# Attention: issue orders of TensorE, ScalarE and VectorE written over two pairs of units, and 1920 columns masked by GpSimd in place of 1792

## The reference, cut to what matters

```python
scores = jnp.einsum('bhqd,bhkd->bhqk', q / math.sqrt(HEAD_DIM), k)
scores = scores + attention_bias
scores = jnp.where(src_mask, -jnp.inf, scores.astype(jnp.float32))
probs = jax.nn.softmax(scores, axis=-1).astype(v.dtype)
ctx = jnp.einsum('bhqk,bhkd->bhqd', probs, v)
```

## Time and profile before

| | us |
|---|---|
| median of 3 runs | 3619.0 |
| the profiled execution | 3623.18 |
| its span, first to last instruction | 3621.4 |
| PE busy (share of the span) | 3559.3 (98%) |
| VectorE busy | 2256.5 (62%) |
| ScalarE busy | 2184.5 (60%) |
| GpSimd busy | 2062.6 (57%) |
| mean granted TensorE clock | 0.993 of full speed |

### The profile page before, as it was taken

The page is one execution under the profiler, slowest core; times in us unless marked ns, Lnnn a source line. Parts: engine busy times, 40 slices in busy tenths (PEclk is TensorE's granted clock), DMA queues, the critical chain, the costliest instruction groups (busy, mean ns, idle before and its releaser), DMA issues. The chain is left out here.

```text
span 3621.4 us, 79854 instructions
## 1 busy us (share of the span) xinstructions
PE 3559.3 (98%) x32051; PEld 2451.5 (68%) x32051; DVE 2256.5 (62%) x4503; ACT 2184.5 (60%) x3047; POOL 2062.6 (57%) x782
## 2 busy tenths in 40 slices
PE   7999999999999999999999999999999999999998
PEld 3444468888888888888888888887544444444444
DVE  7676668888888888888888888887211111111102
ACT  2343369999999999999999999998210210110110
POOL 1111169898899989899998899996310110120100
PEclk8999999999999999999999999999999999999999
DMA  5555598888998888988888988887300110111002
GB/s 190 202 186 185 189 394 326 320 332 322 349 371 322 322 321 331 379 339 325 321 321 335 387 330 321 322 320 262 139 24 11 35 35 11 40 55 39 20 24 93
DMA packets 210118, 828.62 MB, mean 229 GB/s; under 512 B 25044, under 2 KB 58964, under 8 KB 134488
## 3 DMA queue, kind: packets, MB, share of 16 engines
q1 hardware_dynamic: 204532, 815.09, 59.7%
q10 hardware_dynamic: 5220, 8.42, 0.6%
HBM read 732.19 MB, written 91.23 MB: 227 GB/s over the span
## 5 line engine op out<-in xcount | busy, mean ns | idle before, releaser
L1196 POOL TENSOR_TENSOR at_tiles<-at_tiles,at_negmask 128x1792 f32<-128x1792 f32 x509 | 1827.8, 3634 | 191.9 <-DMA at_tiles<-in_bias 178.8
L1286 ACT ACTIVATE at_tiles<-at_tiles,at_rmin 128x2048 f32<-128x2048 f32 x512 | 1025.3, 2002 | 58.2 <-DVE at_rmin L1333 57.6
L1232 PE MATMUL at_ps_p<-consts,at_tiles 128*128 128x128 f32 x8192 | 1024.9, 272 | 0.1
L1232 PEld LDWEIGHTS at_ps_p<-consts,at_tiles 128*128 128x128 f32 x8192 | 929.8, 141 | 37.8 <-ACT at_prob_t L1294 0.6
L1294 ACT ACTIVATE at_prob_t<-at_ps_p 128x512 f32<-128x512 f32 x1536 | 831.5, 596 | 128.7 <-PE at_ps_p L1232 127.1
L1333 DVE CUSTOM_DVE_ANT_0 at_tiles<-at_ps_s,at_tiles 128x1024 f32<-128x1024 f32 x512 | 624.7, 1220 | 119.2 <-PE at_ps_s L1213 112.4
L1213 PE MATMUL at_ps_s<-at_k_stack,at_q_stack 128*128 128x512 f32 x2048 | 677.4, 432 | 6.0 <-DVE at_rmin L1333 4.1
L1333 DVE CUSTOM_DVE_ANT_0 at_tiles<-at_ps_s,at_tiles,at_rmin 128x1024 f32<-128x1024 f32 x512 | 657.8, 1285 | 18.8 <-PE at_ps_s L1219 0.5
L1249 PE MATMUL at_ps_c<-at_prob_t,at_v 128*32 128x128 f32 x16384 | 500.3, 274 | 0.6 <-DVE at_ctx_rows L1351 0.6
L1249 PEld LDWEIGHTS at_ps_c<-at_prob_t,at_v 128*32 128x32 f32 x16384 | 431.6, 110 | 43.7 <-issue 43.0
L1710 PE MATMUL ff_ps_m<-ff_w,ff_hid 128*128 128x512 f32 x1024 | 441.8, 593 | 0.0
(11 more groups left out here) (193 smaller groups left out, 2635.3 us busy)
## 6 DMA issues: line engine op xcount, KB each, us to landing
at_tiles<-in_bias SPq DMA_DIRECT2D x512, 1024.0 KB, 7.0
at_k_stack<-k_hi SPq DMA_DIRECT2D x128, 256.0 KB, 5.1
at_k_stack<-k_lo SPq DMA_DIRECT2D x128, 256.0 KB, 5.3
negm<-em_mask_out SPq DMA_DIRECT2D x32, 512.0 KB, 6.6
at_q_stack<-q_hi SPq DMA_DIRECT2D x128, 128.0 KB, 5.1
at_q_stack<-q_lo SPq DMA_DIRECT2D x128, 128.0 KB, 5.2
at_v<-v SPq DMA_DIRECT2D x64, 256.0 KB, 7.8
at_negmask<-negm SPq DMA_DIRECT2D x32, 512.0 KB, 9.7
```

What stands on the lines that cost most here:

```text
L1196: pool.tensor_tensor(tiles[s][:, 0:PCOLS], tiles[s][:, 0:PCOLS], negm[s][:, 0:PCOLS], ALU.add).then_inc(s_pool, 1)
L1232: last = pe.transpose(ps_p[k][:, y * P:(y + 1) * P], tiles[s][:, t * P:(t + 1) * P], ident)
L1286: act.activation(tiles[s][:, :], tiles[s][:, :], ACT.Exp, bias=rmin[:, s, 1:2], scale=-1.0, accum_out=rsum[:, s:s + 1]).then_inc(s_exp, 1)
```

## The change

The width of GpSimd's masking grows from 1792 to 1920 columns, in the embedding stage too, and TensorE's mask matmul shrinks from 256 to 128 columns. The loop bodies of the three engines now cover two pairs, four units (g counts them, u = 4g, pr = 2g), from g = -1; what falls outside the range of units is skipped by a test at the head of each helper. TensorE runs a unit's scores four units ahead of its transposes. V (`pv`) stands before the last chunk of a unit's transposes, with the second half of one unit's scores and the first half of the next behind it. ScalarE takes 13 of 16 chunks, VectorE 3. The tests (`if not 0 <= u < NU: return`, and the same with pr and NP), one in each of the eleven helpers, are left out of the diff here except for the first.

```diff
--- before.py
+++ after.py
...
 
     at = Parts()
     at.early = 3
-    at.pool_columns = S - 256
+    at.pool_columns = S - 128
     at.k_st, at.q_st, at.v_sb, at.tiles, at.negm = [None] * 2, [None] * 2, [None] * 2, [None] * RING, [None] * RING
 
     def kqv(i):
...
     B, S = net.B, net.S
     QB = S // P
     RING = 8
-    PCOLS = S - 256
+    PCOLS = net.at.pool_columns
     HALF = S // 2
     SPAN = RING * P
     QH = S // SPAN
...
             stack = net.consts[:, C_STACK:C_STACK + 2 * HD]
 
             def qk(u, a):
+                if not 0 <= u < NU:
+                    return
                 n, s, b, qh, h = place(u)
                 if s == 0 and a == 0:
                     pe.wait_ge(s_kin[n % 2], 64 * (n // 2 + 1))
...
                 last.then_inc(s_pv, 1)
 
             def parts_sum(pr):
                 pe.wait_ge(s_cxs, pr + 1)
                 pe.matmul(ps_c[:, P:P + 2 * HD], cx_sb[:], stack, start=True, stop=True).then_inc(s_cxm, 1)
 
-            for u in range(2):
-                qk(u, 0)
-                qk(u, 1)
-            for p in range(NP + 2):
-                u = 2 * p
-                if u + 2 < NU:
-                    qk(u + 2, 0)
-                    qk(u + 2, 1)
-                if p >= 2:
-                    parts_sum(p - 2)
-                if p < NP:
-                    transposes(u, (0, 1))
-                    if u + 3 < NU:
-                        qk(u + 3, 0)
-                    transposes(u, (2, 3))
-                    transposes(u + 1, (0,))
-                    if u + 3 < NU:
-                        qk(u + 3, 1)
-                    transposes(u + 1, (1, 2, 3))
-                if 1 <= p <= NP:
-                    pv(p - 1)
+            for g in range(-1, NU // 4 + 1):
+                u, pr = 4 * g, 2 * g
+                transposes(u, (0, 1))
+                qk(u + 3, 1)
+                parts_sum(pr - 2)
+                transposes(u, (2, 3))
+                qk(u + 4, 0)
+                transposes(u + 1, (0, 1, 2))
+                pv(pr - 1)
+                qk(u + 4, 1)
+                qk(u + 5, 0)
+                transposes(u + 1, (3,))
+                transposes(u + 2, (0, 1))
+                qk(u + 5, 1)
+                parts_sum(pr - 1)
+                transposes(u + 2, (2, 3))
+                qk(u + 6, 0)
+                transposes(u + 3, (0, 1, 2))
+                pv(pr)
+                qk(u + 6, 1)
+                qk(u + 7, 0)
+                transposes(u + 3, (3,))
 
         @block.scalar
         def _(act):
             cxv = net.ctx.rearrange("(b q t p) c -> (b q) p t c", p=P, t=RING, q=QH)
 
             def exp(u):
                 s = u % RING
                 act.wait_ge(s_sc, 2 * u + 2)
                 act.activation(tiles[s][:, :], tiles[s][:, :], ACT.Exp, bias=rmin[:, s, 1:2], scale=-1.0,
                                accum_out=rsum[:, s:s + 1]).then_inc(s_exp, 1)
 
             def take(u, c):
                 k, i = bank(u, c)
                 pr, j = divmod(u, 2)
                 after(act, s_pv, pr - 1)
...
                                ACT.Copy).then_inc(s_pe[k], 1)
 
             def store(pr):
                 if (pr // 4) % HEADS == HEADS - 1:
                     act.wait_ge(s_cxo, pr + 1)
                     of = slice(2 * (pr % 4), 2 * (pr % 4) + 2)
                     act.dma_start(cxv[pr // (4 * HEADS)][:, of, :], cx_all[:, of, :]).then_inc(s_st[pr % 4], 16)
 
-            exp(0)
-            for p in range(NP + 3):
-                u = 2 * p
-                if 1 <= p <= NP:
-                    take(u - 1, 1)
-                if p < NP:
-                    exp(u + 1)
-                    for c in range(3):
-                        take(u, c)
-                    if u + 2 < NU:
-                        exp(u + 2)
-                    take(u + 1, 2)
-                    take(u + 1, 3)
-                if p >= 3:
-                    store(p - 3)
+            for g in range(0, NU // 4 + 1):
+                u, pr = 4 * g, 2 * g
+                take(u - 2, 2)
+                take(u - 2, 3)
+                exp(u)
+                take(u - 1, 1)
+                exp(u + 1)
+                take(u - 1, 3)
+                take(u, 0)
+                take(u, 1)
+                take(u, 2)
+                take(u, 3)
+                exp(u + 2)
+                take(u + 1, 1)
+                take(u + 1, 2)
+                exp(u + 3)
+                take(u + 1, 3)
+                take(u + 2, 0)
+                take(u + 2, 1)
+                store(pr - 3)
+                store(pr - 2)
+            store(NP - 1)
             for i in range(RING // 2):
                 act.wait_ge(s_st[i], 16 * B * QH)
 
...
                                 rinv[:].unsqueeze(2).broadcast_to([P, 2, HD]), ALU.mult).then_inc(s_cxo, 1)
 
             def parts(pr):
                 dve.wait_ge(s_pv, pr + 1)
                 v.tensor_copy(cx_sb[:], ps_c[:, 0:P]).then_inc(s_cxs, 1)
 
-            for u in range(2):
-                scores(u, 0)
-                scores(u, 1)
-            scores(2, 0)
-            for p in range(NP + 2):
-                u = 2 * p
-                if u + 2 < NU:
-                    scores(u + 2, 1)
-                if p >= 2:
-                    context(p - 2)
-                if p < NP:
-                    take(u, 3)
-                    take(u + 1, 0)
-                if u + 3 < NU:
-                    scores(u + 3, 0)
-                    scores(u + 3, 1)
-                if 1 <= p <= NP:
-                    parts(p - 1)
-                if u + 4 < NU:
-                    scores(u + 4, 0)
+            for g in range(-1, NU // 4 + 1):
+                u, pr = 4 * g, 2 * g
+                context(pr - 2)
+                scores(u + 3, 1)
+                scores(u + 4, 0)
+                take(u + 1, 0)
+                parts(pr - 1)
+                scores(u + 4, 1)
+                scores(u + 5, 0)
+                context(pr - 1)
+                scores(u + 5, 1)
+                scores(u + 6, 0)
+                take(u + 3, 2)
+                take(u + 3, 0)
+                scores(u + 6, 1)
+                parts(pr)
+                scores(u + 7, 0)
 
 
 def ffn_stage(nc, net):
```

More of the change, by code:

```diff
@@ L1235, in pv @@
             def pv(pr):
+                if not 0 <= pr < NP:
+                    return
                 n = pr * 2 // RING
```

## The result

The changed kernel takes 3608.8 us, the median of 6 runs, against 3619.65 for the kernel before on the same chip: a ratio of 0.9969, 95% interval 0.9959 to 0.9978, which is 8 to 15 us saved. The forecast was 3611, 8 us less than before; measured are 11 us less.

A forecast was written before the change was run, and what follows sets the result against it. PE was taken to bound attention, with two resources close behind. Terms -19 + 0 + 4 + 7 = -8 took the profiled 3623.2 to 3615, on the median 3611 us; own range 3602 to 3618, whole range 3584 to 3632.

The forecast's parts named there:

- The loop PE, DVE, PE: Attention, each pair: PE's score weight load waits for DVE's minimum; new order removes about 0.075 us a pair, -19 us.
- the tightest place: New attention order: scores(u+7,0) on DVE, parts queued ahead, finish 0.15 us before PE wants them for qk(u+8,0).
- The narrower mask at 0: PE's mask matmul in attention: 128 fewer columns save 0 us; other end 0.053 per mask, -27 us.
- GpSimd: Masking in attention: 1920 columns take 3.90 us, 3.86 a unit back to back, under PE's 3.93; steady-state cost 0.
- The start, +4: Start of attention: looking four units ahead costs 4 us, bounds 0 and 7.
- the two reasons given: Start of attention: POOL no longer catches up; transposes end 14.4 us after their scores begin instead of 10.8.
- The mask reloads, +7: After each of three mask reloads in attention, tiles land late for the scores: 7 us, bounds 3 and 15.
- of which DVE's idle time takes 0.4: After mask reloads: DVE's idle time absorbs only 0.4 us of the 1.8 and 3.9 us shortfalls.
- the 3.9 us by which tiles were to be late: After the third mask reload: masked tiles 3.9 us short of their scores, from 3.2 us of room before.
- the 6.6 and 0.5 taken off: Room between masking and scores after reloads: 6.6 us less from looking further ahead, 0.5 for two longer maskings.
- The starving ring: Rival, chance 0.17: a head's second bias tile comes late, DVE's scores wait in each head; +24 us, 3635.
- The chance of 0.21 for slower: Whole kernel: chance of a measurably slower result, from ring starvation and a quarter of the case where the wait moves.

## Why the prediction was right, and where its terms were off

**The loop PE, DVE, PE** (the step -19). Right: the pair went from 7.93 to 7.86, the wait is what the orders removed, and moving one line removes it too (3606.75). It was a little too large: 0.065 us a pair on the average, 17 us. The term had a bound of 0 because I gave the tightest place 0.15 us. The trace has 0.43 there, and the run with the longer parts bears it out. The error is in VectorE's durations, each a little long: 0.10 in the second half of scores ahead of parts (1.20 for 1.30), 0.09 in parts (0.21 for 0.30), 0.05 in the first half up to its minimum (1.22 for 1.27); the rest is in the layout. The 1.27 of the earlier trace rows is the distance to the unit's own second half, which by the program waits for the first half's minimum. In the new order other work stands between the two, and behind a first half it starts after 1.15.

**The narrower mask at 0.** Right: the run with the old width has the same time, and where a transpose follows a mask the same change saves 0.05 each (3606.1 in the old order, 3582.0 with both masks). So what decides is what follows the mask. That it is the length of the next weight load fits the load records, which were the right row to go by since the distance of 0.12 could not tell; no run varied the load alone. Of the two statements of the Trainium skill ("TensorE: Matmul & The Clock Gate") that I set beside it, the 107 ns for any 128 columns of weights (section LDWEIGHTS) would have made 0 of both masks in every order. A transpose right behind a mask at 0.07 speaks against it for these transposes' weights; that mask and sum take 0.29 at either width agrees with it for the others.

**GpSimd.** 3.87 us measured for 3.90, waiting 14.7 us of 600, no bound. Right.

**The start, +4.** The size was near, and of the two reasons given one was right. Counting transposes in the trace, unit 4's first starts 24.0 us after the first score matmul before, 27.2 after, and 26.9 in the new orders with the old width. So of the 3.2 us GpSimd's catching up has 0.3 at most. The rest came with the orders and is near the other reason, transposes that end 14.4 us behind the start of their scores in place of 10.8, 3.6 us later. The waits of 488 to 560 us show VectorE waiting for GpSimd 13.1 us in the changed kernel:

```profile
DVE at_tiles L1357 <- POOL at_tiles L1196: 13.1, 11, 3.7
```

**The mask reloads, +7.** Much too dear; this is the term that failed. The ring did lose room (the late reads show how little is left), and after the first reload VectorE does wait for GpSimd, 7.5 us in 982 to 1045. But TensorE hardly lost anything:

```profile
DVE at_tiles L1357 <- POOL at_tiles L1196: 7.5, 8, 1.4
```

```profile
1000.22 1.48 PE L1236 MATMUL at_ps_p<-consts,at_tiles 128*128 128x128 f32 x12
...
1063.62 1.47 PE L1236 MATMUL at_ps_p<-consts,at_tiles 128*128 128x128 f32 x12
...
2007.90 1.37 PE L1236 MATMUL at_ps_p<-consts,at_tiles 128*128 128x128 f32 x11
...
2070.83 1.37 PE L1236 MATMUL at_ps_p<-consts,at_tiles 128*128 128x128 f32 x11
```

These are the same place of the loop four groups apart, after the first and the third reload: 63.40 and 62.93 us, where four groups take 4 x 2 x 7.871 = 62.97 by the average pair. So 0.4 us was lost in the first and nothing in the third, where I had reckoned 1.4 and 3.5. Two steps are wrong. For the first reload it is "of which DVE's idle time takes 0.4": VectorE has an idle time of 1.33 and one of 0.52 us in each group, spent on waiting for TensorE, and a late tile uses them before it costs anything. For the third it is the 3.9 us by which tiles were to be late: VectorE waited for GpSimd 0.3 us in 1985 to 2075. The smallest distance there from the end of a masking to its scores went from 3.2 us to nothing and no further, so less room was lost at that place than the 6.6 and 0.5 taken off; why is open.

The starving ring did not come. The run with late reads shows that its mechanism exists: 45 us for reads 2.5 to 5.4 us later, part of it perhaps by late K. The place that I had named, a head's second bias tile, is not what it shows: there the scores start right behind their masking in seven of the eight places of a head.

**The sum.** With what the traces show for each term it is -16.6 + 0 + 3.2 + 0.4 = -13.0, and the two profiled executions differ by 12.8 us from the first score matmul to the end of the kernel. The medians differ by 11 (8 to 15), the forecast by 8. That 3611 lies 2 us from the measured 3608.8 is in part luck: the reload term was 6.6 us too dear and the loop term 2 us too good, and 2 us are less than the scatter between runs. The chance of 0.21 for slower adds up to 0.23 from its own parts.

## What to carry to other kernels

When an engine is busy throughout, compare the start-to-start distance of the same few instructions at two places of the loop: a wait that no view names shows as a difference of hundredths, and one moved line can be worth a rewritten order. A matmul that gets shorter may pay only in front of some instructions: here the mask paid in front of transposes, whose weight loads have the shorter records (0.14 us against 0.19 to 0.20), and not in front of the others; so try what follows it. And when an order looks further ahead, count what that takes from the ring that feeds it: it may cost nothing at once and leave no room for the next delay. And go through every buffer again for every order that you vary: one bank that I had not looked at again cost 361 us in the run with V behind.

## What the runs showed of the hardware that I had not expected

The record of a mask matmul in front of a score matmul is followed by the next start after 0.04 us whether it is 128 or 256 columns wide, while the group of four takes the same 1.16: such a start alone doesn't tell what the mask costs. A first half of scores on VectorE, 1024 columns, costs 1.27 us from start to start when the half that depends on it comes next, and 1.15 when other work does; a second half costs 1.20 to 1.21. A copy of 128 columns that records 0.29 costs 0.20 behind another.
